# Another order table for the merge of five step streams in a transformer-block kernel

## Chip, cores and metric

One Trainium2 chip, one of its cores. The metric is the device time of one execution in microseconds (us). The engines are PE (TensorE), DVE (VectorE), ACT (ScalarE), POOL (GpSimd) and SP (SyncE, which issues the DMAs).

## What is computed

Four batches `b` of 512 rows by 128 columns go through four residual layers. In the reference, cut to what matters:

```python
x = x + xattn16(layernorm(x), ctx_768)        # 16 heads of 8 columns against 77 keys
x = x + moe(layernorm(x))                     # 8 experts, hidden 512, top 2 of 8 weigh them
x = x + text_block(layernorm(x), ctx_768)     # below
x = x + int8_matmul(layernorm(x), rhs)        # rows and rhs quantized to int8

def text_block(x_text, x_vision):
    scores = einsum('bthd,bghd->bhtg', Q, K) / sqrt(32)   # 4 heads
    topv, topi = top_k(scores, 32)                        # 32 of 77, softmax, mean of the heads
    c_t = attn_mean @ V
    x = layernorm(x_text) * (1 + g * scale_in) + g * shift_in
    y = s4d(x)                                            # convolution by a generated kernel, as FFT
    xt = x_text + y * (1 + g * scale_out) + g * shift_out
    xt = xt + gelu(layernorm(xt) @ W1 + b1) @ W2 + b2
    return layernorm(xt)
```

## The kernel before

The kernel is written as 690 steps `(kind, batch, index)`. Each engine's program is one loop over the same list `order`, in which it does its own part of each step. So the list sets the order within each engine's queue, and semaphores set the rest: a step that does nothing on an engine takes no place in its queue.

There are five streams, each with a fixed inner order. H (226 steps) has the setup and, by batch, the 16-head attention (`ln_stats`, `ln_apply`, `norm_T`, `q_proj`, two parts of `q_split`, `v_place`, four `smax`, `smax_T`, sixteen pairs of `score` and `pv`, two `attn_sum`, `attn_norm`, `o_proj`) and the router up to `b2_add`. E (256) has the expert matmuls, `moe_up` and `moe_down` by expert and quarter, 64 for each batch. T (128) has the text attention (`norm_T`, `text_q`, four rounds of `topk` for each of four row tiles, `topw`, `am_T`, `film`). O (64) has what follows (`dft`, `spectrum`, `idft`, `s4_out`, the feed-forward part `ffn_up` and `ffn_down`, three layer norms, and `quant`, `quant_T`, `quant_mm`, which ends in the store). K (16) makes the convolution kernel: five setup steps, `kgen_base`, four pairs of `kgen_tables` and `kgen_mm`, `kgen_dft`, `kgen_spec`.

The table ORDER merges them: `H9 K5` means nine steps of H, then five of K. `plan` (its `needed` holds what must go before what) turns it into the list, and `place_fills` hands the four PSUM banks called `side` to the steps in the list's order, leaving out a bank held by the sum of eight `pv` steps. The experts have PSUM banks of their own, two for `moe_h` and two for `moe_y`.

What sets the order of work around the places that matter here:

- `q_split` makes three bfloat16 pieces of Q. ScalarE makes the first from `qs` (L914), VectorE the residual (L1048), ScalarE the second (L917), VectorE the third (L1051). SP copies them within SBUF to the tile QA with twelve DMAs (L601), six for the first piece, four for the second, two for the third, and PE's first `smax` (L688) waits for all twelve.
- `smax` gives the row maxima for `score` (PE L703), whose exponential (ACT L932) `pv` (PE L713) reads.
- `moe_up` is PE L759 and ACT L950; `moe_down` is PE L771, and VectorE adds its result to X at the fourth quarter (L1170).
- `dft` (PE L811, ACT L974), `spectrum` (VectorE L1235 to L1253 and POOL beside it), `idft` (PE L822, VectorE L1258).
- `kgen_tables` is a chain over VectorE (L1370 to L1382), ScalarE and POOL (L1526 to L1534); POOL starts it only when PE has done the `kgen_mm` (L859) of the piece before.
- `norm_T` is PE L636, `text_q` L778, `am_T` L792, `film` L799, `ffn_up` L830, `ffn_down` L838, `attn_norm` L721, `o_proj` L728, `w_T` L741 (it reads L1155 of `route_w`), `b2_add` L748.

Of the kernel before, what the change touches and what calls it, by code (L numbers as in the profile page):

```python
# [16 lines left out]
T = S // P  # L17
# [12 lines left out]
E8, HC = 8, 4  # L30
# [105 lines left out]


ORDER = """
H9 K5 H5 K H16 K H11 K H2 K H9 K H K H5 E H E H E2 H E H3 K E6 K E4 H3 E H E H E5 H E3 K H2 E2 H10 K2 H8 E H E3 H13
E5 H E2 H3 E7 H E H2 E2 H E2 H E2 H3 E7 H E H3 E5 H T E9 T2 E H E3 H T H E H E T3 E2 H E9 H2 T3 E H2 T2 H9 T H3 E H  # L140
T3 E H E H3 E T H T H E H2 E H5 T H2 T7 E H E7 H T H E T2 H2 E H E6 H E H3 T E5 H E2 H2 E2 T H E5 T2 H E H3 E2 H O T
E2 O E7 H T E H T H E H O H T2 E3 T O2 E4 H3 T H E H9 T H T H3 E H E3 H8 O H2 T3 H5 T3 H E4 T2 O E2 T2 E O E T5 O2 H
E8 O2 T H E O T E2 T E3 T O T E6 H E5 H O E4 T H T2 H2 E2 O2 H2 E T2 O H E2 T E2 T3 E T O E6 T E O E3 O E5 O T4 E O
E3 O T5 E2 T2 E4 T4 E3 O2 T E T E2 O T O E6 T O T E7 T E O E11 T3 O3 T3 O T3 O3 T O T O T4 O T11 O T2 O T O T2 O T2
O2 T O18
"""


# [1459 lines left out]
```

## Time and profile before

| | us |
|---|---|
| median of three runs | 654.06 (653.02 to 655.34) |
| the profiled execution | 655.16 |
| its span in the profile | 653.4 |
| PE busy | 511.7 (78%) |
| VectorE busy | 453.3 (69%) |
| ScalarE busy | 239.2 (37%) |
| POOL busy | 135.2 (21%) |
| DMA, of 16 engines' span | 8.9% |

The page is read from its shares of busy time to its slices, which show where in the span an engine is full. In a timeline row the first number is the start and the second the time it covers, in us from the span's start; behind it stand the engine, the line of the kernel, the operation, what is written and read with shapes, how many instructions the row merges, and in brackets the engine's idle time ahead of it and what ended it. "PEld" are PE's weight loads and "SPq" the issues of DMAs.

### The profile page before, as it was taken

The page shows a single profiled execution, that of the slowest core. Times are in us where ns is not written, and L with a number is a line of the kernel's source. Part 1 is how long each engine was busy: PE and PEld are TensorE (multiplying, and loading weights), DVE is VectorE, ACT ScalarE, POOL GpSimd, SP SyncE. Part 2 cuts the span into 40 slices and gives each one's busy share as a digit, 9 for nine tenths or more (in the row PEclk, how much of TensorE's full clock was granted, in tenths as well). Part 3 has the DMA queues.
Part 4 walks back from the last instruction along what each step waited for, and adds up shares of the span by engine and source line. Part 5 has one row for each costly group of instructions (what it writes and reads, how often), then busy time and mean ns, then how long its engine had stood idle before and what let it go on. Part 6 is the DMA issues. An engine that isn't in the chain of part 4 may idle for free.

```text
span 653.4 us, 8060 instructions
## 1 busy us (share of the span) xinstructions
PE 511.7 (78%) x2539; PEld 310.9 (48%) x2539; DVE 453.3 (69%) x1771; ACT 239.2 (37%) x406; POOL 135.2 (21%) x164
## 2 busy tenths in 40 slices
PE   3539545298999999999999999999999964825360
PEld 2111113256445766445776435776767743413230
DVE  7369456557144546968669877988989879996516
ACT  3324551455433343444343446334363410401020
POOL 3502435333100010001132001215011152112210
PEclk9967665587999999999999999999999997776785
DMA  4509100011000030000012000000000000000000
GB/s 125 118 10 336 35 0 1 1 28 23 4 0 1 1 42 9 3 1 2 0 21 30 2 2 0 2 2 17 1 2 2 1 17 1 2 1 16 0 1 16
DMA packets 16156, 14.18 MB, mean 22 GB/s; under 512 B 1290, under 2 KB 14354, under 8 KB 16114
## 3 DMA queue, kind: packets, MB, share of 16 engines
q1 hardware_dynamic: 16114, 13.68, 8.6%
q8 instruction: 20, 0.33, 0.2%
q14 instruction: 22, 0.18, 0.1%
HBM read 8.86 MB, written 1.05 MB: 15 GB/s over the span
## 4 chain that ended last, share of the span: by engine, by line
PE 61%; DVE 21%; issue 4%; SPq 4%; DMA 4%; ACT 3%; POOL 2%; POOLq 0%; DVEq 0%
PE moe_y L771 16%; PE moe_h L759 15%; PE side L713 7%; SPq L601 4%; DMA QA<-Q 4%; PE side L822 3%; PE side L811 2%; PE side L703 2%; PE side L830 2%; PE side L838 2%; DVE area L1194 2%; PE side L799 1%; PE side L688 1%; PE side L636 1%; DVE TOP L1184 1%
## 5 line engine op out<-in xcount | busy, mean ns | idle before, releaser
L771 PEld LDWEIGHTS moe_y<-W,HT 128*128 128x128 f32 x1024 | 131.1, 193 | 45.6 <-issue 44.2
L771 PE MATMUL moe_y<-W,HT 128*128 128x128 f32 x1024 | 135.3, 277 | 0.0
L759 PE MATMUL moe_h<-xnT_moe,W 128*128 128x512 f32 x256 | 134.4, 614 | 0.0
L950 ACT ACTIVATE HT<-moe_h,W 128x512 f32<-128x512 f32 x128 | 87.4, 686 | 118.9 <-PE moe_h L759 118.7
L713 PE MATMUL side<-PT,VP 128*72 128x512 f32 x128 | 72.8, 655 | 10.6 <-ACT PT L932 10.6
L932 ACT ACTIVATE PT<-side 77x512 f32<-77x512 f32 x64 | 37.4, 591 | 45.9 <-PE side L703 45.6
L1170 DVE SCALAR_TENSOR_TENSOR X<-moe_y,RW,X 128x128 f32<-128x128 f32 x128 | 35.9, 342 | 20.7 <-PE moe_y L771 20.5
L759 PEld LDWEIGHTS moe_h<-xnT_moe,W 128*128 128x128 f32 x256 | 40.8, 196 | 12.4 <-issue 7.5
L1455 POOL TENSOR_TENSOR area<-area 128x128 f32<-128x128 f32 x16 | 7.3, 456 | 164.4 <-ACT area L967 164.4
L1194 DVE MATCH_REPLACE8 area<-TOP,area 128x77 f32<-128x77 f32 x192 | 40.5, 222 | 0.0
L703 PE MATMUL side<-QA,KA 50*77 50x512 bf16 x64 | 25.6, 428 | 14.4 <-ACT qs L936 8.0
L703 PEld LDWEIGHTS side<-QA,KA 50*77 50x77 bf16 x64 | 6.7, 111 | 61.7 <-issue 52.4
L1110 DVE TENSOR_REDUCE mx<-side 128x6 f32<-128x462 f32 (+1 forms) x48 | 24.5, 577 | 15.4 <-PE side L688 15.3
L1184 DVE MAX8 TOP<-area 128x8 f32<-128x77 f32 x192 | 31.2, 224 | 0.0
L822 PE MATMUL side<-area,FI 128*128 128x256 f32 x64 | 17.9, 442 | 14.6 <-DVE area L1253 14.3
L713 PEld LDWEIGHTS side<-PT,VP 128*72 128x72 f32 x128 | 14.8, 149 | 28.9 <-issue 17.3
L1120 DVE RECIPROCAL xT_head<-side 8x512 f32<-8x512 f32 x4 | 13.4, 3355 | 18.3 <-PE side L713 18.3
L688 PE MATMUL side<-KM,QA 128*128 128x154 bf16 x128 | 15.4, 267 | 9.7 <-DMA QA<-Q 9.7
L822 PEld LDWEIGHTS side<-area,FI 128*128 128x128 f32 x64 | 14.1, 226 | 17.7 <-issue 15.3
L958 ACT ACTIVATE area<-area 128x308 f32<-128x308 f32 x16 | 7.4, 460 | 36.7 <-DVE area L1187 36.6
L799 PE MATMUL side<-FF,AMT 78*128 78x512 f32 x32 | 17.7, 635 | 3.9 <-ACT AMT L961 3.9
L811 PE MATMUL side<-area,FW 128*128 128x256 f32 x80 | 20.6, 416 | 0.0
(307 smaller groups left out, 835.7 us busy)
## 6 DMA issues: line engine op xcount, KB each, us to landing
W<-in_w SPq DMA_DIRECT2D x8, 512.0 KB, 7.8
QA<-Q SPq DMA_DIRECT2D x48, 64.0 KB
X<-in_x SPq DMA_DIRECT2D x4, 256.0 KB, 6.2
out_dram<-FO SPq DMA_DIRECT2D x4, 256.0 KB, 2.3
V<-in_vpack SPq DMA_DIRECT2D x1, 579.0 KB, 3.6
area<-in_r2pack SPq DMA_DIRECT2D x1, 576.0 KB, 7.0
area<-in_gpack SPq DMA_DIRECT2D x1, 576.0 KB, 4.5
FW<-in_dftf SPq DMA_DIRECT2D x1, 512.0 KB, 7.3
```

The costliest lines, as they stand in the source:

```text
L601: sp.dma_start(QA[r0:r0 + HD0, :, :], Q3[64 * u:64 * u + 64, piece, :]).then_inc(q_spread, 16)
L703: pe.matmul(dst[0:NK, :], KA[r0:r0 + SROWS, i // 2, b * NK:(b + 1) * NK], QA[r0:r0 + SROWS, i // 2, :], start=True, stop=True).then_inc(fu ...
L713: mm = pe.matmul(dst[0:GROWS, :], VP[:, g, GROWS * h:GROWS * (h + 1)], PT[:, i % NPT, :], start=(h == 0), stop=(h == HG - 1))
L759: pe.matmul(moe_h[n % 2][:], W1[:, e, c * P:(c + 1) * P], xnT_moe[:, b % 2, :], start=True, stop=True).then_inc(moe_h_full, 1)
L771: mm = pe.matmul(moe_y[m % 2][:, t * P:(t + 1) * P], HT[:, m % 2, c, t * P:(t + 1) * P], W2[:, e, c, :], start=(c == 0), stop=(c == HC - 1))
L811: mm = pe.matmul(dst[:, q * 2 * D:(q + 1) * 2 * D], FW[:, k, (2 * n + q) * P:(2 * n + q + 1) * P], src[:, k::2, :], start=(k == 0), stop=( ...
L822: mm = pe.matmul(dst[:, half * 2 * D:(half + 1) * 2 * D], FI[:, r, half * P:(half + 1) * P], y, start=(r == 0), stop=(r == 3))
L932: act.activation(PT[0:NK, i % NPT, :], src[0:NK, :], ACT.Exp).then_inc(read, 1)
L950: act.activation(HT[:, m % 2, c, :], moe_h[n % 2][:], ACT.Relu, bias=wc("b1")[:, e * HC + c:e * HC + c + 1]).then_inc(moe_h_ready, 1)
L1170: ins = dve.scalar_tensor_tensor(X[:, b, t, :], moe_y[m % 2][:, t * P:(t + 1) * P], RW[:, b % 2, t, e:e + 1], X[:, b, t, :], ALU.mult, ALU ...
L1184: dve.max(TOP[:, a, h, r, :], s).then_inc(top_max, 1)
L1194: dve.match_replace(TW[:, h, :], TOP[:, a, h, r, :], s, PICKED)\
```

## The change

Only the table differs. The streams, each step's instructions and the other functions stay, so both lists hold the same 690 steps, and the assignment of the `side` banks follows the new order. Where steps come to stand otherwise:

- the five setup steps of K stand ahead of `v_place` of batch 0, the first `kgen_mm` behind the `pv` and `score` steps that followed it, the second ahead of `ln_stats` of the experts' norm; the third `kgen_tables` stays; `kgen_dft` and `kgen_spec` stand three to five steps of H later;
- in batch 1 the expert steps are spread among the heads, and 36 instead of 31 of them stand ahead of its last `pv`;
- between the second `q_split` and the first `smax` stand 9, 12 and 8 expert steps in batches 1, 2 and 3, which were 10, 15 and 11;
- `dft`, `spectrum` and `idft` of batch 0 stand ahead of batch 3's first `q_split`, and `s4_out` ahead of its second; they were behind both;
- batch 3's `smax_T` and its scores stand behind 156 to 169 expert steps and 47 to 53 text steps, which were 143 to 150 and 36 to 39; `ffn_up` of batch 0 stands ahead of them;
- behind the last expert step the same steps stand in nearly the same order.

```diff
--- before.py
+++ after.py
@@ -136,13 +136,13 @@
 
 
 ORDER = """
-H9 K5 H5 K H16 K H11 K H2 K H9 K H K H5 E H E H E2 H E H3 K E6 K E4 H3 E H E H E5 H E3 K H2 E2 H10 K2 H8 E H E3 H13
-E5 H E2 H3 E7 H E H2 E2 H E2 H E2 H3 E7 H E H3 E5 H T E9 T2 E H E3 H T H E H E T3 E2 H E9 H2 T3 E H2 T2 H9 T H3 E H
-T3 E H E H3 E T H T H E H2 E H5 T H2 T7 E H E7 H T H E T2 H2 E H E6 H E H3 T E5 H E2 H2 E2 T H E5 T2 H E H3 E2 H O T
-E2 O E7 H T E H T H E H O H T2 E3 T O2 E4 H3 T H E H9 T H T H3 E H E3 H8 O H2 T3 H5 T3 H E4 T2 O E2 T2 E O E T5 O2 H
-E8 O2 T H E O T E2 T E3 T O T E6 H E5 H O E4 T H T2 H2 E2 O2 H2 E T2 O H E2 T E2 T3 E T O E6 T E O E3 O E5 O T4 E O
-E3 O T5 E2 T2 E4 T4 E3 O2 T E T E2 O T O E6 T O T E7 T E O E11 T3 O3 T3 O T3 O3 T O T O T4 O T11 O T2 O T O T2 O T2
-O2 T O18
+H8 K5 H6 K H16 K H13 K2 H7 K H3 K H7 E4 H E H3 K E6 K E H E2 H E H E H E3 H E3 H E3 K E H E2 H E H13 K E2 H2 K E4 H3
+E H13 E H E4 H E3 H2 E7 H E H E H E2 H E2 H E H E H3 E7 H E2 H2 E H2 T E10 T E T E H E H E H E T H E T E H T2 E9 T
+H2 T E3 T3 H T E2 H13 T4 H2 E4 H3 T H T H11 T4 E H T E3 H T3 E H T2 H E H E9 H T E H3 E4 T H T H3 E2 O2 E2 T E2 H E
+H E O H O E H E2 O T E4 H E2 T2 H E H T E H E3 O H E2 T O2 T2 E5 T2 E T4 E T E H T E2 O E2 T4 E4 T E5 H2 T4 O E3 H4
+T H11 E O E H4 E H2 E H2 O H8 T4 O T H E3 O H T E3 O H2 O H O E2 O E4 H E5 T H3 E2 O H E T H T E3 T O E O T4 E9 O E2
+O T E2 T3 E4 O E T2 E T5 E3 T O T E O T2 E4 T E6 T2 E O E9 O T2 O E T E4 O T E8 T3 O2 T O2 T5 O T O T O T6 O2 T4 O
+T6 O T2 O T2 O2 T3 O20
 """
 
 
```

## Rows read from the trace of the kernel before

**Rows 1.** The page, part 1: busy us, share of the span and instructions.
```profile
PE 511.7 (78%) x2539; PEld 310.9 (48%) x2539; DVE 453.3 (69%) x1771; ACT 239.2 (37%) x406; POOL 135.2 (21%) x164
```

**Rows 2.** Windows: start and end, length, busy us (instructions) by engine, PEclk, DMA, GB/s.
```profile
163.00:526.00 363.00, 358.08 (x1863) 225.56 (x1861) 260.07 (x1170) 153.45 (x265) 48.70 (x74) 1.00 0.04 6
526.00:591.00 65.00, 33.04 (x114) 20.59 (x114) 61.34 (x315) 13.81 (x28) 18.60 (x23) 0.75 0.02 5
591.00:653.40 62.40, 25.48 (x94) 16.94 (x94) 30.07 (x89) 6.66 (x10) 10.11 (x11) 0.66 0.03 9
```

**Rows 3.** Timeline of PE: two `moe_up` with a `moe_down` between.
```profile
343.37 1.02 PE L759 MATMUL moe_h<-xnT_moe,W 128*128 128x512 f32 x2
...
345.12 1.02 PE L759 MATMUL moe_h<-xnT_moe,W 128*128 128x512 f32 x2
```

**Rows 4.** Timeline around the first `kgen_mm` and the second `kgen_tables`.
```profile
62.79 0.49 DVE L1375 TENSOR_SCALAR area<-area,C 128x512 f32<-128x512 f32 x1
63.31 0.43 DVE L1376 TENSOR_SCALAR area<-area 128x512 f32<-128x512 f32 x1
...
79.98 2.20 PE L859 MATMUL side<-area 128*32 128x16 f32 x64
...
82.11 1.08 PE L713 MATMUL side<-PT,VP 128*72 128x512 f32 x2
...
82.39 1.29 DVE L1375 TENSOR_SCALAR area<-area,C 128x512 f32<-128x512 f32 x1
...
83.72 2.01 DVE L1376 TENSOR_SCALAR area<-area 128x512 f32<-128x512 f32 x1
...
95.00 1.13 PE L713 MATMUL side<-PT,VP 128*72 128x512 f32 x1 [9.13 <-ACT PT L932]
```

**Rows 5.** Timeline at batch 1's first `smax`, and the window behind it.
```profile
149.38 1.02 PE L759 MATMUL moe_h<-xnT_moe,W 128*128 128x512 f32 x2
153.31 2.41 PE L688 MATMUL side<-KM,QA 128*128 128x154 bf16 x16 [2.91 <-DMA QA<-Q]
...
153.30:159.60 6.30, 6.29 (x34) 5.11 (x35) 5.36 (x13) 4.78 (x6) 2.35 (x3) 0.50 0.00 0
```

**Rows 6.** Timeline, batch 2: `q_proj` and the first `smax`.
```profile
232.24 1.10 PE L679 MATMUL side<-xT_head,W 128*128 128x512 f32 x2
...
248.62 0.58 PE L688 MATMUL side<-KM,QA 128*128 128x154 bf16 x6 [1.35 <-DMA QA<-Q]
```

**Rows 7.** Timeline, batch 3 and the transform of batch 0, and a window.
```profile
335.52 1.10 PE L679 MATMUL side<-xT_head,W 128*128 128x512 f32 x2
...
338.09 8.01 SPq L601 DMA_DIRECT2D QA<-Q  x12
338.17 3.62 PE L811 MATMUL side<-area,FW 128*128 128x256 f32 x16
...
350.51 0.42 DVE L1253 TENSOR_TENSOR area<-area 128x256 f32<-128x256 f32 x1
...
351.09 0.72 PE L688 MATMUL side<-KM,QA 128*128 128x154 bf16 x8 [1.44 <-DMA QA<-Q]
...
344.00:347.00 3.00, 3.00 (x20) 2.29 (x19) 3.00 (x4) 1.37 (x2) 2.92 (x4) 1.00 0.57 72
```

**Rows 8.** Timeline of PE: steps that stand close behind what they read.
```profile
368.95 1.05 PE L713 MATMUL side<-PT,VP 128*72 128x512 f32 x2 [0.77 <-ACT PT L932]
...
526.35 1.10 PE L799 MATMUL side<-FF,AMT 78*128 78x512 f32 x2 [0.45 <-ACT AMT L961]
...
534.11 1.10 PE L778 MATMUL side<-area,V 128*128 128x512 f32 x2 [0.83 <-ACT area L904]
```

**Rows 9.** Windows: 88 to 136 us.
```profile
88.00:136.00 48.00, 22.63 (x109) 13.05 (x110) 26.54 (x62) 15.19 (x22) 20.26 (x15) 0.50 0.00 1
```

**Rows 10.** Timeline: the last of `route_w` and its reader `w_T`, batch 3.
```profile
449.13 0.19 DVE L1155 TENSOR_TENSOR RW<-RS,RZi 128x32 f32<-128x32 f32 x1
...
450.02 0.60 PE L741 MATMUL side<-C,RW 128*8 128x128 f32 x4
```

## Prediction

> **What bounds the kernel now.** I read the page's busy shares first [rows 1], then the stages. PE is busy for 358.1 of 363 us between 163 and 526 us, at the granted clock 1.00: there the experts' matmuls and all side work stand in one PE queue and nothing but PE's order and its few waits counts [rows 2]. From 526 to 591 us VectorE bounds (61.3 of 65 us busy), and after that the last batch's chain runs alone. In the first 163 us a chain of dependent steps bounds, and PE runs at half its clock for much of it [rows 9]. So I ask three things of the new table: does the start chain change, does PE wait more or less between 163 and 526 us, does the end change.
>
> The span is 653.4 us and this execution took 655.16, 1.8 around the span; the median of the runs is 654.06, 1.1 below. I sum against 655.16 and take off 1.1.
>
> **What the change moves.** No step is added or removed, so each engine's instructions are the same in number and kind. Walking both tables step by step, with PE's starts read from the trace (an expert's up and down piece together 1.75 us, 0.88 each [rows 3]; every other pair of neighbours likewise), PE's work from the last generation matmul to the last expert piece comes to 350.0 us in either order: new neighbours cost nothing. What is left is waits.
>
> *Moves without a price.* `v_place` of batch 0 behind the five setup steps stands on POOL's queue alone, and its reader comes 20 us later. The second `kgen_mm` passes `ln_stats` and `ln_apply`, which have nothing on PE or ScalarE; the first expert pieces pass the same two steps of batch 1. Each engine's own order stays as it is. Price 0. The attention heads of batch 1 get expert pieces spread among them: PE has the same work, and the steps behind them that read VectorE's results gain 4 to 6 us of room. Price 0.
>
> *First `kgen_mm` behind two more attention steps: -0.7.* It starts at 79.98 and takes 2.2 us [rows 4]. In the new table one `pv` (1.08 us) and one `score` (some 0.3) go ahead, so it ends about 1.2 us later, and POOL, which waits for it, starts its two products later. VectorE's chain is what the attention behind it waits for, and there two instructions that take 0.49 and 0.43 us when POOL rests took 1.29 and 2.01 beside those products: 2.4 us lost [rows 4]. Later products miss them and fall on L1377 to L1380 instead. If only L1380 is hit, 1.4 us is won; if the two-input ones are hit as well, nothing. I take the middle, -0.7, between -1.4 and 0 (a further loss of about 0.5 is possible).
> The Trainium skill (SBUF — State Buffer, "SBUF: two separate sides") says the port pair that VectorE and GpSimd share is an exclusive lock, and that a VectorE instruction with two SBUF inputs takes it too, against a GpSimd one that reads SBUF. By that the products hit L1377 and L1379 as hard as before, and this term would be 0 and the sum 0.7 higher.
>
> *Batch 1, `q_split` to `smax`: +0.9.* PE waits here for the QA copies, from the end of the matmul at 149.38 (about 1.02 long) to 153.31 [rows 5]. Those copies set the moment; the new table has one expert step less ahead of it (9, not 10), which PE then does later: 0.88 more wait.
>
> *Batch 2, the same place: +1.4.* From `q_proj` (232.24) to the first `smax` (248.62) 16.4 us pass [rows 6]; 15.1 in batch 1 and 15.6 in batch 3 [rows 7]. Ahead of it stood 15 expert steps, 14.5 us of PE work with the two others; now 13 expert steps, 12.8 us. Against a chain of 15.6 PE waits 2.8 us (2.3 to 3.6), where it waited 1.4.
>
> *Batch 3, the transform of batch 0 goes ahead of `q_split`: +2.0.* Now `dft`, `spectrum` and `idft` of batch 0 stand before batch 3's `q_split`, `idft` and `s4_out` between its parts. `spectrum` ends 12.8 us after `dft` starts (338.17 to 350.93), whatever PE does [rows 7]. The new table has 10.3 us of PE work between `dft` and `idft`: six expert steps 5.3, `dft` 3.5, a transpose and `q_proj` 1.4. PE waits 2.4 us, with all behind it. VectorE's residual of Q now comes after `idft`'s reading: `dft`+12.8, `idft` 3.7, reading and residual 1.4, ScalarE's second piece 0.6, that is `dft`+18.6; six of the twelve copies remain. Twelve take 13.0 us from first issue to reader, and at the 72 GB/s of [rows 7] one of 64 KB is 0.9 us, so six take about 7.8: `dft`+26.4. PE gets there at `dft`+12.8+12.7+1.0 = 26.5 (`idft` 3.5, nine expert steps 7.9, a transpose and `text_q` 1.3, and 0.8 to 1.0 for `text_q` standing right behind its transpose [rows 8]). PE's waits here sum to 3.5 against 1.5 before [rows 7], +2.0; if the copies are no faster for being fewer, 5.1, +3.6.
>
> *Pairs that stand close.* PE no longer waits 0.8 for the exponential at batch 3's first `pv` [rows 8], for expert steps stand between: -0.8. Three pairs become neighbours: `am_T` and `film` (0,3) 0.2 and (1,0) 0.45, `norm_T` and `ffn_up` of batch 0 about 0.9 by the like waits of [rows 8]: +1.6.
>
> *VectorE in the middle: +1.2.* Text batch 1 now goes almost wholly ahead of batch 3's scores, `ffn` of batch 0 about 33 us of PE work earlier and the heads of batch 3 16 later. Counting VectorE's work ahead of each reader the same way, the readers `am_T` (1,0) to (1,2), `attn_norm` 3 and `norm_T` ffn lose 12 to 17 us of a slack of 12 to 16: near zero, and PE's new waits before give back 2 to 3. Behind `spectrum` of batch 1 VectorE has to get through the routing weights of batch 3, which came only 0.7 us before their PE reader [rows 10], and the text normalization of batch 2, now with 3 us less room for both. I take 0.4 + 0.8, from 0 to 3.
>
> *The end.* Behind the last expert piece both tables hold the same steps, and VectorE reaches it with nothing queued in either. There VectorE is full, its sum does not change, and the last step before the final chain (`topw` 3, then `ln_apply` and `quant` of batch 2) is the same. 0, within 1 for `ffn_up` of batch 2, now 9 us later, with 1.7 us left before its reader.
>
> Sum: -0.7+0.9+1.4+2.0-0.8+1.6+1.2 = +5.6. 655.16+5.6 = 660.8; less 1.1, **659.7**.
>
> **Rivals.** *The clock falls.* At batch 1's wait PE stood for 2.9 us and the clock then was 0.50 for 6.3 us of solid matmuls [rows 5]; the waits of 1.4 us in batches 2 and 3 left it at 1.00. With 2.8 us in batch 2 it may fall again: half of 6.3, +3.1, 662.8. The Trainium skill (TensorE: Matmul & The Clock Gate, "Part 1: The HAM clock gate") has the array gated to half rate after idling; this trace agrees.
> *The waits only change places.* Low ends throughout: -1.4+0.9+0.8+0.6-0.8+0.5 = +0.6, 654.7. This needs copies that land as soon as they are few, and VectorE never late. The steady 15.1 to 16.4 us speak against it.
> *VectorE is late* over text batch 1 and the routing of batch 3: some 4 us more, 664.
> *Faster: the clock rises at the start.* Place: 88 to 136 us, 22.6 us of PE work at 0.50 [rows 9], nearly all on the chain. If the denser `pv`, `score`, `kgen_mm` ahead of it kept PE at full clock, up to half of that, 11 us, is won, less the 6.3 of my other terms: 649.4. It decides from 6.3 us won, a granted clock over about 0.8 there. Against it: PE still stands for 9.1 us, till 95.00, for that chain [rows 4], and 0.50 began about then.
> That the table does nothing is excluded: the queues differ in order.
>
> **Chances.** Forecast 0.42, clock falls 0.18, VectorE late 0.08, change of places 0.20, faster 0.12. A measurement tells about 0.3%, 2 us, from no change: faster 0.12, within 0.20, slower 0.68. The range goes from the change of places with a little below to VectorE late with a little above: 653 to 665; the likeliest case alone 657.5 to 662.
>
> **What would show it.** PE waits for QA copies of about 3.8, 2.8 and under 1.5 us at the first `smax` of batches 1 to 3; a wait of about 2.4 for VectorE's L1253 at the `idft` of batch 0; the last expert piece at about 530 instead of 525 us; about 128 us from there to the end, as now. Wrong if PE has less than 5 us of idle time in that stage, if the stretch behind the last expert piece changes by over 2 us, or if the clock of 88 to 136 us is not 0.50.

## The result and the profile after

The changed kernel takes 664.11 us (median of four runs, 660.63 to 664.16) against 654.02 (653.02 to 655.34): a ratio of 1.014, with a 95% interval of 1.010 to 1.018. It is slower by 10 us. The forecast was 659.7, in a range of 653 to 665: sign and range held, the size was short by 4.4. The profiled execution took 664.16, with a span of 662.4 against 653.4: +9.0.

The page's busy shares after, to be read against [rows 1]; the engines do the same instructions.

```profile
PE 517.8 (78%) x2539; PEld 312.9 (47%) x2539; DVE 452.2 (68%) x1771; ACT 239.2 (36%) x406; POOL 136.6 (21%) x164
```

Windows of the changed kernel: start and end, length, busy us (instructions) of PE, PEld, DVE, ACT, POOL, then PEclk, DMA, GB/s. The first answers to [rows 9], the next three to [rows 2] with their borders moved by what PE is late.

```profile
88.00:136.00 48.00, 22.62 (x110) 13.02 (x111) 26.58 (x61) 15.73 (x24) 20.95 (x16) 0.54 0.00 1
163.00:532.00 369.00, 360.67 (x1863) 227.62 (x1862) 260.11 (x1172) 153.55 (x264) 49.35 (x74) 0.99 0.03 6
532.00:597.00 65.00, 33.97 (x122) 20.47 (x120) 59.42 (x307) 13.71 (x27) 18.61 (x23) 0.73 0.02 5
597.00:662.40 65.40, 26.67 (x95) 17.43 (x95) 32.14 (x97) 6.93 (x11) 10.12 (x11) 0.66 0.03 8
254.50:261.30 6.80, 5.90 (x29) 4.62 (x30) 3.14 (x6) 0.04 (x1) 0.00 (x0) 0.50 0.00 0
348.60:355.00 6.40, 6.38 (x31) 5.03 (x32) 5.00 (x19) 1.25 (x3) 3.44 (x6) 1.00 0.30 63
```

In the full stage PE is idle for 8.3 of 369 us, where it was idle for 4.9 of 363. The granted clock there is 0.99 and not 1.00: the fifth window, behind batch 2's first `smax`, ran at 0.50. From 88 to 136 us it reads 0.54 where I had said 0.50: the clock fell at 90.7 us instead of 87.9, but PE had no matmul between 88.0 and 90.6, so nothing is won or lost by it.

Timeline rows of PE, changed kernel (start, duration, engine, line, what, and in brackets the idle time ahead and its releaser), with VectorE's last of `spectrum` and the QA copies' issues. They answer to [rows 5], [rows 6], [rows 7] and [rows 8].

```profile
153.78 1.21 PE L688 MATMUL side<-KM,QA 128*128 128x154 bf16 x8 [4.56 <-DMA QA<-Q]
...
255.40 1.21 PE L688 MATMUL side<-KM,QA 128*128 128x154 bf16 x8 [3.12 <-DMA QA<-Q]
...
335.75 3.62 PE L811 MATMUL side<-area,FW 128*128 128x256 f32 x16
...
347.51 10.79 SPq L601 DMA_DIRECT2D QA<-Q  x12
...
348.09 0.43 DVE L1253 TENSOR_TENSOR area<-area 128x256 f32<-128x256 f32 x1
...
348.62 3.69 PE L822 MATMUL side<-area,FI 128*128 128x256 f32 x16 [2.43 <-issue]
...
361.53 1.10 PE L778 MATMUL side<-area,V 128*128 128x512 f32 x2 [0.92 <-ACT area L904]
362.46 0.71 PE L688 MATMUL side<-KM,QA 128*128 128x154 bf16 x8
...
373.54 3.67 PE L830 MATMUL side<-xT_tail,V 128*128 128x512 f32 x8 [0.96 <-ACT xT_tail L902]
...
384.33 1.10 PE L799 MATMUL side<-FF,AMT 78*128 78x512 f32 x2 [0.80 <-issue]
```

All the waits that the prediction placed are there: QA copies at the first `smax` of batches 1 and 2, none in batch 3, L1253 at `idft`, and the close pairs. I compare starts of steps in both traces and take off what a pair of neighbours costs without a wait; a wait comes out 0.1 to 0.2 us longer by this than the idle time in its row's brackets. That gives this account, in us:

| stretch | before to after | forecast |
|---|---|---|
| start, up to batch 1's `q_proj` | -0.3 | -0.7 |
| batch 1, `q_proj` to the last generation matmul | +1.1 | +0.9 |
| an expert step, not `score`, behind that matmul | -0.9 | none |
| batch 2, wait for QA (1.5 to 3.2) | +1.8 | +1.4 |
| batch 2, clock 0.50 behind it | +2.7 | none (the rival) |
| batch 3, `idft` +2.6, QA wait -1.6, close `text_q` +1.1 | +2.1 | +2.0 |
| `pv` 0 of batch 3 | -0.8 | -0.8 |
| `ffn_up` +1.1, `film` (1,0) +1.0 | +2.1 | +1.6 |
| VectorE in the middle | 0 | +1.2 |
| the rest, gaps of neighbours under 0.25 us | -0.7 | 0 |
| behind the last expert piece | +1.9 | 0 |
| sum | +9.0 | +5.6 |

### The profile page after: what moved, and what is told of

The parts are those of the page before. It is cut to its first block, busy times and chain, and to the rows that moved or that the text cites. A ratio compares the mean times of both kernels' runs of the same rounds, so it can differ in the third digit from the quotient of the medians.

```text
span 662.4 us, 8060 instructions
## 1 busy us (share of the span) xinstructions
PE 517.8 (78%) x2539; PEld 312.9 (47%) x2539; DVE 452.2 (68%) x1771; ACT 239.2 (36%) x406; POOL 136.6 (21%) x164
## 4 chain that ended last, share of the span: by engine, by line
PE 63%; DVE 21%; issue 5%; SPq 3%; ACT 3%; DMA 3%; POOL 2%; POOLq 0%; DVEq 0%
PE moe_y L771 16%; PE moe_h L759 16%; PE side L713 7%; SPq L601 3%; PE side L822 3%; PE side L811 3%; DMA QA<-Q 3%; PE side L703 2%; PE side L830 2%; PE side L838 2%; DVE area L1194 2%; PE side L799 2%; PE side L688 1%; PE side L636 1%; DVE TOP L1184 1%
## 5 line engine op out<-in xcount | busy, mean ns | idle before, releaser
L713 PE MATMUL side<-PT,VP 128*72 128x512 f32 x128 | 74.8, 673 | 8.7 <-ACT PT L932 8.7
L822 PE MATMUL side<-area,FI 128*128 128x256 f32 x64 | 20.2, 486 | 16.7 <-DVE area L1253 14.3
L713 PEld LDWEIGHTS side<-PT,VP 128*72 128x72 f32 x128 | 14.7, 151 | 25.7 <-issue 14.9
L1120 DVE RECIPROCAL xT_head<-side 8x512 f32<-8x512 f32 x4 | 13.4, 3355 | 19.2 <-PE side L713 19.2
L822 PEld LDWEIGHTS side<-area,FI 128*128 128x128 f32 x64 | 15.9, 253 | 21.6 <-issue 18.6
L688 PE MATMUL side<-KM,QA 128*128 128x154 bf16 x128 | 15.4, 275 | 10.7 <-DMA QA<-Q 10.3
L830 PE MATMUL side<-xT_tail,V 128*128 128x512 f32 x32 | 19.4, 764 | 1.9 <-ACT xT_tail L902 1.9
```

The lines of the kernel that those rows point to most:

```text
L713: mm = pe.matmul(dst[0:GROWS, :], VP[:, g, GROWS * h:GROWS * (h + 1)], PT[:, i % NPT, :], start=(h == 0), stop=(h == HG - 1))
L822: mm = pe.matmul(dst[:, half * 2 * D:(half + 1) * 2 * D], FI[:, r, half * P:(half + 1) * P], y, start=(r == 0), stop=(r == 3))
L830: pe.matmul(dst[:], vc("w1f")[:, c * P:(c + 1) * P], xnT["ffn"][:], start=True, stop=True)\
```

## Experiments

Each kernel differs from the changed one or the one before in its table alone; the diffs show a piece of the table, a letter being a stream and the number how many steps of it. Medians are each against the kernel before on the same chip. One kernel's runs spread by 2 to 7 us, so the accounts below are read from the traces' starts of steps. There is one trace of each kernel. Three of them have before's table up to batch 1: their starts agree within 0.3 us up to its `q_proj`, but its wait for the QA copies was 2.91, 3.77 and 3.77 us, so a difference below 1 us at such a wait shows nothing.

**Two more expert steps ahead of batch 2's smax** (changed table, behind `norm_T` of text batch 0):

```diff
-T E H E H E H E T H E T E H
+T E3 H E H E H T E H T H
```

> The changed table, with two more expert steps ahead of each of the four smax of batch 2 (14 instead of 12 between its second q_split and its first smax), else the same. In the changed kernel PE waited 3.2 us there for the QA copies and the granted clock was 0.50 for 6.8 us behind it. Theory 'the wait pulls the clock down': the wait shrinks by two steps, 2 x 0.88 = 1.75 us, to about 1.5 us, the clock stays at 1.00 there, and the last expert piece comes 1.75 + 2.7 = 4.4 us sooner than in the changed kernel. Rival 'the clock falls there for another reason' (for instance which steps stand close to each other): only 1.75 us sooner, with 0.50 still there. Rival 'the copies come sooner too or are hit by something else': the wait stays near 3 us and nothing is won.

Timeline and windows of this kernel: the first `smax` of batch 2, the stretch behind it, and the stretch behind `idft`.

```profile
254.86 0.72 PE L688 MATMUL side<-KM,QA 128*128 128x154 bf16 x8 [1.61 <-DMA QA<-Q]
...
254.00:261.00 7.00, 5.58 (x42) 3.93 (x43) 5.56 (x13) 1.12 (x2) 0.00 (x0) 1.00 0.00 0
345.20:352.00 6.80, 6.80 (x25) 5.40 (x26) 3.74 (x17) 0.53 (x1) 2.89 (x6) 0.75 0.28 59
```

The wait went from 3.1 to 1.6 us and the clock stayed at 1.00. From batch 2's `q_proj` to batch 3's this kernel is 2.6 us quicker, not 4.4: 1.5 of wait and 2.7 of clock were won, but in this order `text_q` and `smax_T`, now nearer to what they read, wait 1.1 and 0.7. At `idft` the same wait as in the changed kernel now was followed by 0.50 for half of the window, 1.7 us. The last expert piece came 1.74 sooner, of which 0.8 from the start. The whole: 662.6, ratio 1.010 (1.004 to 1.016).

**The suspected cause alone: two expert steps fewer there, in the kernel before:**

```diff
-E2 T2 E H E3 H T H E H E T
+E T2 H E3 H T H E H E3 T
```

> The kernel before, with two expert steps fewer ahead of each of the four smax of batch 2 (13 instead of 15 between its second q_split and its first smax), else the same. The suspected cause alone. Theory 'a wait of about 3 us pulls the clock down': PE waits 1.35 + 1.75 = 3.1 us there, the granted clock falls to 0.50 for some 6.8 us, and it takes 1.75 + 2.7 = 4.4 us longer than before. Rival 'the clock has another cause': the wait alone, 1.75 us longer, the clock 1.00 throughout 163 to 526 us.

Timeline row and window of this kernel (its lines stand one lower, L687 is L688).

```profile
248.87 1.21 PE L687 MATMUL side<-KM,QA 128*128 128x154 bf16 x8 [2.64 <-DMA QA<-Q]
...
248.40:251.80 3.40, 2.93 (x17) 2.94 (x18) 1.57 (x3) 0.00 (x0) 0.00 (x0) 0.55 0.00 0
```

The wait grew from [rows 6]'s 1.35 to 2.64, and 0.50 came with it. From `q_proj` of batch 2 to `smax_T` this is 3.7 us longer than before: 1.3 for the wait, 1.4 for the clock (the two steps behind it took 0.46 and 0.90 more than at 1.00), and 1.0 because two later `smax` now stand closer to VectorE's maxima. The stretch at 0.50 was 3.4 us, half of what was expected. The whole is 660.65, ratio 1.008 (1.004 to 1.011), although the table is that of before but for two steps; the rest of the trace's 6.6 us is 0.7 ahead of batch 2 and 2.2 behind the last expert piece. The clock fell with the longer wait, and the steps ahead of it are the same but for the two that now stand behind it: in this pair of traces the wait brings it. It doesn't do so each time, as the run with the close pairs parted shows below.

**`idft` three expert steps later** (changed table):

```diff
-H E O H O E H E2 O T
+H E4 O H O H O T
```

> The changed table, with the idft of batch 0 behind three more expert steps, which stood behind it, else the same. In the changed kernel PE waited 2.6 us there for spectrum. Theory of the prediction: the moment of idft is set by spectrum, 12.8 us after dft; the three steps (2.6 us) fill the wait, idft starts at the same distance from dft, and PE comes 2.6 us sooner to batch 3's first smax. Its QA copies were written by 360.5 us and PE came at 362.5, so up to 0.7 us is given back there as a wait: the last expert piece 1.9 to 2.6 us sooner. Rival 'the wait is nothing but the first of two': the copies are the next thing late, the wait for QA is over 2 us, and less than 0.6 us is won.

Rows of PE, ScalarE and SP of this kernel.

```profile
347.89 3.62 PE L822 MATMUL side<-area,FI 128*128 128x256 f32 x16
...
362.70 1.21 PE L688 MATMUL side<-KM,QA 128*128 128x154 bf16 x8 [2.77 <-DMA QA<-Q]
...
348.67 0.62 ACT L914 ACTIVATE Q<-qs 128x512 bf16<-128x512 f32 x1
...
349.38 8.11 SPq L601 DMA_DIRECT2D QA<-Q  x12
```

The wait at `idft` is gone and another of the same size stands at `smax`, with 0.50 behind it: this kernel is 3.6 us slower in batch 3 than the changed one (667.3, ratio 1.017). The rival was right, for a reason that neither side named. `q_split` stood behind the three expert steps, so ScalarE made the first piece (L914) behind their activations, 13.9 us after `dft` and not 11.1, and the copies began 2.8 us later behind `dft` than in the changed kernel. First issue to reader was 13.3 us.

**Both `q_split` ahead of those three steps:**

```diff
-H E O H O E H E2 O T
+H E H2 E3 O3 T
```

> The changed table, with both q_split of batch 3 ahead of the three expert steps and these ahead of the idft of batch 0 (in the run with the idft three steps later alone, ScalarE made the first piece of Q 1.9 us later, behind the exponentials of those steps, and PE waited 3.0 us for the QA copies). Theory 'the copies take 13 us from their first issue, whatever their residual waits for': the first issue is at about 1.4 us behind q_proj's expert step as in the changed kernel, the copies are there when PE comes, both waits are gone, and the last expert piece comes 2.3 to 2.6 us sooner than in the changed kernel. Rival 'the residual, behind spectrum on VectorE, sets the copies': a wait for QA of 1.5 to 2.5 us at batch 3's first smax takes the place of the one at idft, and under 1 us is won.

The same four rows of this kernel.

```profile
349.83 3.62 PE L822 MATMUL side<-area,FI 128*128 128x256 f32 x16
...
361.23 0.71 PE L688 MATMUL side<-KM,QA 128*128 128x154 bf16 x8
...
347.82 0.62 ACT L914 ACTIVATE Q<-qs 128x512 bf16<-128x512 f32 x1
...
348.52 8.72 SPq L601 DMA_DIRECT2D QA<-Q  x12
```

Neither step waits. From batch 3's `q_proj` to its `smax_T` 2.2 us are won, as the first theory had it (661.7, ratio 1.007, 1.004 to 1.010). The residual still came behind `spectrum`, and the copies were there 12.7 us after their first issue all the same. But the residual was hardly late for them: in batch 2 of the changed kernel SP comes to the seventh issue, the first that needs the residual, 4.0 us after the first one, and here that took 4.9 us, in the run before this 4.2. So these two runs show that ScalarE's first piece times the copies while the residual is less than 1 us late for its issue. In the changed kernel it was later, which is taken up below.

**Close pairs parted** (changed table; `text_q`, `ffn_up`, `film` in turn):

```diff
-T2 H E H T E H
+T E T H E H T H
...
-T O2 T2 E4
+T O E O T2 E3
...
-T3 E T
+T2 E T2
```

> The changed table, with one expert step put between norm_T and text_q of text batch 1, between norm_T and ffn_up of batch 0, and between am_T and film of row tile 0 of text batch 1 (and one between the first two smax of batch 3, so that they don't become neighbours). PE waited 1.08, 1.12 and 0.97 us in these pairs in the changed kernel, 3.2 in all. Theory: a pair costs what its copy by ScalarE takes, and one step of 0.88 us hides most of it: 3 x 0.88 = 2.6 us are won at the last expert piece. Rival 'the waits are slack that the next wait eats' (VectorE's maxima and top-k results are due at fixed times behind): less than 1 us is won, and PE waits longer at a topk, am_T or smax behind.

Two of the steps, and two windows: behind `idft`'s wait (2.4 us) and behind batch 2's first `smax`, where PE had waited 3.2 us.

```profile
359.19 1.10 PE L778 MATMUL side<-area,V 128*128 128x512 f32 x2
...
370.37 3.67 PE L830 MATMUL side<-xT_tail,V 128*128 128x512 f32 x8
...
344.70:348.10 3.40, 3.40 (x9) 2.75 (x10) 2.25 (x13) 0.00 (x0) 0.96 (x1) 0.54 0.38 90
254.20:261.00 6.80, 6.78 (x55) 5.15 (x56) 6.36 (x15) 1.28 (x2) 0.00 (x0) 1.00 0.00 0
```

The waits of 1.08, 1.12 and 0.97 shrank to 0, 0.26 and 0. From batch 3's `q_proj` to its `smax_T`, where all three stand, 0.9 us is won although the clock behind `idft` took 1.7 there, so 2.6 by the pairs, as expected. The last expert piece came 4.9 sooner, but 2.8 of that is batch 2's clock, which stayed at 1.00 here behind the same wait, 1.3 came at the start, and the clock behind `idft` took 1.7 back. The whole: 661.5, ratio 1.009 (1.007 to 1.012).

**Batch 1 filled** (kernel before):

```diff
-H3 E H E H E5 H E3 K H
+H E3 H2 E H E H E4 H E K H
```

> The kernel before, with three more expert steps ahead of each of the four smax of batch 1 (and two more ahead of its smax_T), else the same. There PE waited 3.0 us for the QA copies and stood at 0.50 for 6.3 us after it. Theory 'the wait pulls the clock down': three steps fill 2.6 us of the wait, 0.4 us is left, the clock stays at 1.00, and the score and pv steps behind come 2.6 + 3.1 = 5.7 us sooner than before, as does the last expert piece. Rival 'the clock has another cause' (it was 0.50 until 147 us and has just risen): only 2.6 us sooner and 0.50 still there. Rival 'the chain of VectorE's maxima bounds batch 1': smax_T waits, under 1 us is won.

Rows of PE and ScalarE of this kernel.

```profile
157.36 2.08 PE L759 MATMUL moe_h<-xnT_moe,W 128*128 128x512 f32 x2 [6.27 <-ACT HT L950]
...
147.44 1.28 ACT L989 ACT_TABLE_LOAD   x1
...
152.79 1.06 ACT L993 ACTIVATE area<-area 128x1024 f32<-128x1024 f32 x1 [2.91 <-DVE area L1382]
...
156.64 1.25 ACT L950 ACTIVATE HT<-moe_h,W 128x512 f32<-128x512 f32 x2
```

No theory held: `smax` came 7.6 us later, and the whole took 663.3, ratio 1.012. ScalarE is in the chain of the third generation piece from 147.4 to 156.6 us (two table loads, and 2.9 us for VectorE) and runs no expert activation. With two `moe_h` banks PE can put out two more `moe_up`; the third, which I had put ahead of `smax`, waited for that chain, and `smax` behind it. Both tables stop short of it.

**All of before's waits filled, and all of the changed kernel's.** Batches 2 and 3 as here (and `pv` 0 parted), or as in the runs above with three steps for batch 2; batch 1 with three and four more:

```diff
-T E H E3 H T H E H E T3 E2 H E
+T E3 H E3 H T H E H T3 E2 H
...
-E H T E H T H E H O
+E3 H T E H T H E H O
```

> The kernel before, with three more expert steps ahead of batch 1's smax (as in the run above), two more ahead of those of batches 2 and 3 (waits of 1.5 and 1.6 us), and one between score 1 and pv 0 of batch 3 (0.84 us). Theory: every wait of PE between 163 and 526 us is worth its length at the end of that stage: 5.7 + 1.5 + 1.6 + 0.8 = 9.6 us sooner than before at the last expert piece, and as much in the whole, about 645 us, if the stretch behind is as long as before. Rival 'the tail gives it back': VectorE, full from 526 us on, has the same work left and the last piece's lead is lost: 2 to 5 us won in the whole. Rival 'waits only change places': less than 3 us won at the last expert piece, with new waits at smax_T, topk or pv.

> The changed table with all of its waits filled: four more expert steps ahead of batch 1's smax, three more ahead of batch 2's, both q_split of batch 3 ahead of idft and three expert steps, and the three close pairs parted. Theory: the sum of the waits and of the two stretches at 0.50 behind them, 3.6 + 3.1 in batch 1, 2.6 + 2.7 in batch 2, 2.6 at idft, 3.2 in the pairs less 0.6 that stay, goes: 17 us at the last expert piece against the changed kernel, that is at about 515 us, 10 sooner than before and within 1 us of the kernel before with its waits filled. So the table's own order (text and transform of batch 0 ahead of batch 3's scores) costs nothing; only its waits do. Rival 'the order costs': VectorE or ScalarE is late in batch 3 once PE doesn't wait, and it stays 3 us or more behind the filled kernel before.

Both ran into the same stop in batch 1 (659.1 and 660.3; ratios 1.006 and 1.008) and lost 6.5 and 6.2 us there. Behind it before's table won 0.9 in batch 2 and 2.2 in batch 3, the changed one 5.1 and 4.8.

**The same with batch 1 right.** One step more ahead of batch 1's `smax` in before's table and two in the changed, the next `moe_up` left behind three `smax` on end:

```diff
-H3 E H E H E5 H
+H E H3 E H E5 H
...
-H E2 H E H E H E3 H E3 H
+H E4 H3 E3 H E3 H
```

> The kernel before, with one expert step more (not three) ahead of batch 1's first smax, so that three smax run on end and the expert step behind them is moe_up (2,2) as before; batches 2 and 3 and the pv as in the run that filled all. In that run moe_up (2,2) stood ahead of smax and waited 6.3 us: ScalarE was in the third generation piece's chain and freed no HT and moe_h till 156.6 us. Theory 'ScalarE's chain is the limit of batch 1, and only there': moe_up (2,2) waits for nothing over 0.5 us, 0.9 us of wait goes in batch 1, and the last expert piece comes 0.9 + 0.9 + 2.2 = 4.0 us sooner than before; if the 2.2 us of wait that is left in batch 1 doesn't pull the clock down, 7 us. The whole is 647 to 650 us. Rival 'the pieces of batches 2 and 3 only won time because batch 1 was late': less than 1.5 us are won.

> The changed table with its waits filled as before, but with two expert steps more (not four) ahead of batch 1's first smax and three smax on end. In the run that filled all, batch 1 lost 6.3 us at moe_up (2,2) and batches 2 and 3 won 5.1 and 4.8. Theory 'the table's order is sound, its waits are the loss': 1.75 + 5.1 + 4.8 = 11.7 us sooner than the changed kernel at the last expert piece, that is at about 520 us, 4.6 sooner than the kernel before, and within 1.5 us of the kernel before with its own waits filled. Rival 'the order costs by itself': 3 us or more behind that kernel.

Rows: before's table, the `score` behind the third generation piece's matmul with a window there; the changed table, batch 2's first `smax`.

```profile
171.10 0.41 PE L702 MATMUL side<-QA,KA 50*77 50x512 bf16 x2 [0.85 <-issue]
...
170.00:173.30 3.30, 2.45 (x18) 2.16 (x16) 0.00 (x0) 2.14 (x6) 1.66 (x2) 0.72 0.02 5
...
254.24 0.72 PE L688 MATMUL side<-KM,QA 128*128 128x154 bf16 x8 [0.42 <-DMA QA<-Q]
```

The changed table takes 653.67 with its waits filled, 10.4 less than as it was given (on another chip), ratio 0.997 (0.995 to 0.999) against the kernel before, which was 1.014. Its last expert piece starts at 520.7, 11.1 sooner than in the changed kernel (1.1, 5.2 and 4.8 by batch). Before's table takes 652.92, ratio 0.996 (0.995 to 0.997). Each beats both kernels, by little; the two are within 0.8 us of each other. So the new order as such costs no more than about 1 us; the waits that it opened cost the rest. Batch 1 disappointed: the copies time its `smax` (153.4 us), and in before's table a stretch at 0.50 at 171 us, behind a wait of 0.85, took 1.7. So before's last expert piece came only 1.4 us sooner than in the kernel before, not 4.0: batches 2 and 3 won 3.1 and batch 1 lost 1.7.

**Batches 2 and 3 alone in before's table:**

> The kernel before with batches 2 and 3 filled (two expert steps more ahead of their smax, one between score 1 and pv 0 of batch 3) and batch 1 left as it was. In the run with one step more in batch 1, PE was 0.1 us late at batch 1's smax_T and the clock was 0.50 once more behind the third generation matmul, which cost 1.7 us. Theory 'the clock there is chance, the edit in batch 1 is worth nothing': batches 2 and 3 win 0.9 + 2.2 = 3.1 us at the last expert piece, and the whole is 651 to 652 us, as good as that run or 1 us better. Rival 'batch 1 must be late for the others to win': under 1.5 us are won at the last expert piece.

The last expert piece comes 2.6 us sooner (3.1 won in batches 2 and 3, 0.5 lost ahead of them, where the table is that of before), but the whole takes 653.4, ratio 0.998 (0.997 to 1.000): in the profiled execution the stretch behind it was 2.2 us longer. Whether the edit in batch 1 adds anything stays open; by the traces it adds nothing.

## Why the prediction came out so

*Right in mechanism and size:* four of the waits. Batch 2's is 3.2 less 1.5, `idft`'s is 2.6 (2.4 forecast), `smax` of batch 3 doesn't wait, `pv` saves 0.8. The last expert piece starts at 531.8, with the clock's 2.7 taken off at 529.1, where about 530 was said.

*Batch 1: right sum, partly by luck.* I had a wait of 3.8 us, and it is 4.56: the reader came 13.3 us after the copies' first issue, where the trace before has 12.5, and in the two other traces with before's table up to there it was 13.4. So my 12.5 was a quick case. The longer copies and the step less make 1.7; 0.6 came back because PE spent 1.7 us of the stretch at 0.50 (152.1 to 158.9 us) waiting, and before only 0.6 us. That leaves +1.1.

*The copies of batch 3: as forecast, and met by luck.* I had them ready at `dft`+26.4, timed by a residual that stands behind `idft`'s reading. Rows of the changed kernel: the residual, the last six issues, and windows up to the last packet of the copies and behind it.

```profile
353.02 0.68 DVE L1048 TENSOR_TENSOR qr<-qs,Q 128x512 f32<-128x512 f32 x1
354.44 3.87 SPq L601 DMA_DIRECT2D QA<-Q  x6
...
354.44:360.76 6.32, 6.17 (x36) 4.21 (x34) 5.69 (x23) 2.61 (x4) 2.12 (x5) 1.00 0.40 62
360.76:362.40 1.64, 0.87 (x2) 0.40 (x3) 0.00 (x0) 0.63 (x2) 0.00 (x0) 1.00 0.00 0
```

The seventh issue came at `dft`+18.7 (18.6 forecast), 6.9 us behind the first one and not 4.0, and the last packet ended at `dft`+25.0. In six waits for these copies in three traces PE started 0.9 to 1.5 us behind the last packet, so they were ready at about `dft`+26.2, an estimate. PE came at `dft`+26.7 and just didn't wait. In the run with two more steps in batch 2 the seventh issue was 8.6 us behind the first, and the last packet ended 14.9 us behind it, where it was 12.0 in batch 2 of the changed kernel: a residual that is 3 us late or more does time the copies. That the two came out within 1 us of each other was luck; I had 0.1 us between them.

*What I sized wrong: the clock in batch 2.* I gave it 0.18 and held that a wait of 2.8 us leaves the clock at 1.00, though my one row of a wait of that size [rows 5] was followed by 0.50. Of nine waits of 2.4 to 3.4 us in batches 2 and 3 of the traces taken here, seven were followed by 0.50, which cost 1.4 to 2.7 us each where I took it apart, and two were not; waits up to 1.7 us never were there. Three more, of 2.5 to 2.6 us at 176 us in the runs that stopped in batch 1, were all followed by 0.50. What decides at 2.4 to 3.4 stays open: the same wait of 2.4 at `idft` stayed at 1.00 in the changed kernel and fell in two others. The fastest of the changed kernel's four runs is 3.5 us below the rest, somewhat over this price, but it has no trace, and its mean granted clock of 0.856 against 0.857 doesn't speak for it, so that stays open. The Trainium skill (TensorE: Matmul & The Clock Gate, "Part 1: The HAM clock gate") says that the monitor behind the clock runs free of the kernel's start, so that one kernel comes out differently from run to run. That agrees with one wait of 2.4 us having gone both ways, but no run here shows the monitor itself.

*The start: -0.7 forecast, nothing in this trace.* The second chain of `kgen_tables` in the changed kernel, to be read against [rows 4]: VectorE, then POOL's two products.

```profile
82.52 0.48 DVE L1375 TENSOR_SCALAR area<-area,C 128x512 f32<-128x512 f32 x1
83.04 0.43 DVE L1376 TENSOR_SCALAR area<-area 128x512 f32<-128x512 f32 x1
...
85.49 1.43 DVE L1380 TENSOR_SCALAR area<-area,C 128x1024 f32<-128x1024 f32 x1
86.95 2.28 DVE L1381 TENSOR_SCALAR area<-area 128x1024 f32<-128x1024 f32 x1
...
84.84 1.53 POOL L1526 TENSOR_TENSOR area<-area,C 128x512 f32<-128x512 f32 x1 [4.79 <-PE side L859]
86.45 2.24 POOL L1527 TENSOR_TENSOR area<-area,C 128x1024 f32<-128x1024 f32 x1
```

L1375 and L1376 are quick now, and L1380 and L1381 took 1.43 and 2.28 where they had taken 0.75 and 0.69: 2.3 us lost instead of 2.4, and L1382 starts at 89.27 in both. I had left L1381 out of the products' reach. In the run with the `idft` later the products came a little earlier against the chain:

```profile
83.70 1.96 DVE L1379 TENSOR_TENSOR area<-area,C 128x1024 f32<-128x1024 f32 x1
85.70 2.28 DVE L1380 TENSOR_SCALAR area<-area,C 128x1024 f32<-128x1024 f32 x1
```

L1379, with two inputs from SBUF, took 1.96 there and 1.23 in the changed kernel: 2.3 lost once more. The Trainium skill (SBUF — State Buffer, "SBUF: two separate sides") says that VectorE and GpSimd lock each other out of the shared port pair, and that this holds too for a VectorE operation with two SBUF inputs against a GpSimd one that reads SBUF; by it the term would be 0, and these rows agree. Over all traces the last `pv` of batch 0 starts at 94.5 to 95.0 in the seven of the changed table and its variants and at 94.8 to 95.3 in the six of before's, so some 0.4 may be there; it was gone by batch 1's copies.

*VectorE in the middle: +1.2 forecast, 0.* No reader of VectorE's results waited over 0.25 us there but `idft`. Slacks of 12 to 16 us less 12 to 17 were near zero by my count, and PE's 5 us of new waits ahead of them are what I should have taken off in full; no run tests that.

*The close pairs: 1.12 and 0.97 for `ffn_up` and `film` (1,0), against 0.9 and 0.45.* The third, `film` (0,3), priced at 0.2, has `w_T` between on PE and waited 0.02. I priced `film` by a place of [rows 8] where ScalarE was free. Here it had the exponential of a `topk` ahead, with a table load, and made its copy late:

```profile
382.31 1.28 ACT L958 ACT_TABLE_LOAD   x1
...
383.97 0.26 ACT L961 ACTIVATE AMT<-side 78x128 f32<-78x128 f32 x1
```

*Missed:* behind the last generation matmul PE had waited 0.83 us for the first `score`; the new table has an expert step there.

*The end: 0 within 1 forecast, +1.9.* It doesn't take the new table. In the last chain, rows of the changed kernel, of before with two steps less (its own table there, lines one lower), and of the changed table with two more in batch 2:

```profile
617.71 6.37 PE L822 MATMUL side<-area,FI 128*128 128x256 f32 x16 [9.23 <-DVE area L1253]
632.30 5.91 PE L830 MATMUL side<-xT_tail,V 128*128 128x512 f32 x8 [0.96 <-ACT xT_tail L902]
...
615.35 6.38 PE L821 MATMUL side<-area,FI 128*128 128x256 f32 x16 [9.23 <-DVE area L1252]
...
615.62 5.22 PE L822 MATMUL side<-area,FI 128*128 128x256 f32 x16 [9.22 <-DVE area L1253]
629.05 5.32 PE L830 MATMUL side<-xT_tail,V 128*128 128x512 f32 x8 [0.96 <-ACT xT_tail L902]
```

The same sixteen matmuls take 6.4 or 5.2 us and the same eight 5.9 or 5.3, in either table, by how much of them falls on 0.50. From the last expert piece to the end it was 128.2 to 132.3 us over thirteen traces of the two tables and their variants, on average 130.4 in the seven of the changed table and 129.3 in the six of before's. That difference is well inside the spread of each, so no more than about 1 us of the 1.9 is likely to be the table's, and my ±1 was too narrow.

## What to carry over

Where an in-order engine has work enough, judge a merge order by its waits: between each step that reads over another engine or a DMA and the start of that result, count the independent work, and price a wait of PE with the clock behind it (here 1.4 to 2.7 us more, in seven of nine waits of 2.4 to 3.4 us). Before a filler is moved there, ask what it puts into every other engine's queue: once its activations stood ahead of the step that starts the copies, once behind a chain that freed no buffer, and each cost more than the wait.

## What the hardware showed

- QA's twelve copies of 64 KB: where PE waited for them in batches 1 to 3, it started 12.5 to 13.8 us after their first issue. With the seventh issue 6.9 and 8.6 us behind the first, and not 4.0, the last packet ended 13.2 and 14.9 us behind the first issue, and not 12.0.
- Granted clock 0.50 behind PE waits in batches 2 and 3: seven of nine waits of 2.4 to 3.4 us, none up to 1.7 us. Elsewhere also once behind 0.85 us of wait that followed 64 short matmuls, and once behind 1.28 us just after the last expert piece (at 524.9 us in the changed table with its waits filled).
- VectorE lost 2.3 to 2.4 us to the same two GpSimd products wherever in its chain they fell, and they took up to 1.5 and 2.8 us where they had taken 1.1 and 2.0.
